# State-space chunks: VectorE adds the product with D behind the sums of y, in place of GpSimd's sum with the part from the state

## What is computed

```python
zxbcdt = u @ in_w.T
z, xBC, dt = jnp.split(zxbcdt, [D_INNER, D_INNER + CONV_DIM], axis=-1)
dt = jax.nn.softplus(dt + dt_bias)
xBC = silu(causal depthwise convolution of xBC with 4 taps, + conv_b)
xh, Bm, Cm = jnp.split(xBC, [D_INNER, D_INNER + D_STATE], axis=-1)
dA = jnp.exp(dt * -jnp.exp(A_log))
state = dA_t * state + (dt_t * x_t) B_t          # for every token t
y_t = state C_t
y = ys + Dp * xh                                  # 32 heads of 32 channels
y = y * jax.nn.silu(z)
y = y * rsqrt(mean(y * y) + EPS) * rms_w
return y @ out_w.T
```

## Time and profile before

| what | value |
|---|---|
| median of 3 runs | 1711.53 us (1709.33 to 1713.68) |
| the profiled execution, its own time | 1710.17 us |
| its span, from the first to the last instruction | 1708.4 us |
| busy: PE, DVE, ACT, POOL | 1363.5, 1109.4, 671.5, 417.0 us |
| mean granted clock of PE | 0.871 of full speed |

### The profile page before, as it was taken

One profiled execution on the slowest core, in us unless ns is written; L12 is line 12 of the kernel. 1 busy time (PEld: TensorE's weight loads), 2 busy tenths in 40 slices (PEclk: granted clock), 3 DMA queues, 4 the chain that ended last, 5 costly groups with the idle time before them and its releaser, 6 DMA issues.

```text
span 1708.4 us, 34435 instructions
## 1 busy us (share of the span) xinstructions
PE 1363.5 (80%) x12846; PEld 928.9 (54%) x12847; DVE 1109.4 (65%) x1669; ACT 671.5 (39%) x1011; POOL 417.0 (24%) x390
## 2 busy tenths in 40 slices
PE   3734889888548989884738999976699999999991
PEld 2214566665345666652425555544477777777770
DVE  3586877887578778876876555556456774667432
ACT  3236434344364343341252111124346664566330
POOL 0122333443313434432132323323100000000004
PEclk9757799999778899987858999885799999999996
DMA  8051000000220000003221000005543553535004
GB/s 293 18 173 61 2 2 1 1 1 1 80 82 2 2 1 1 1 1 105 93 83 50 0 0 0 0 4 209 193 183 142 218 217 114 218 126 219 25 25 153
DMA packets 34029, 132.30 MB, mean 77 GB/s; under 512 B 6665, under 2 KB 8457, under 8 KB 24017
## 3 DMA queue, kind: packets, MB, share of 16 engines
q1 hardware_dynamic: 25808, 103.19, 16.7%
q0 software_dynamic: 8160, 28.32, 4.9%
HBM read 108.82 MB, written 22.68 MB: 77 GB/s over the span
## 4 chain that ended last, share of the span: by engine, by line
PE 57%; DVE 24%; issue 7%; ACT 6%; DMA 4%; POOL 2%; DVEq 0%; POOLq 0%; SPq 0%; ACTq 0%
PE banks L2102 13%; PE banks L2123 13%; DVE mb_ca L592 8%; PE banks L1644 6%; PE banks L1003 5%; PE banks L1721 2%; PE banks L977 2%; PE banks L1040 2%; PE banks L1697 2%; PE banks L1050 2%; PE banks L1051 1%; ACT mb_ca L804 1%; POOL xs_table L2135 1%; DVE mb_xc L604 1%; DVE mb_y_lo L640 1%
## 5 line engine op out<-in xcount | busy, mean ns | idle before, releaser
L2102 PE MATMUL banks<-eb_x_hi,eb_w_hi 128*128 128x128 f16 x1344 | 228.3, 220 | 2.0 <-DVE eb_x_lo L2002 2.0
L2102 PE MATMUL banks<-eb_x_lo,eb_w_hi 128*128 128x128 f16 x1344 | 228.3, 220 | 0.0
L2102 PE MATMUL banks<-eb_x_hi,eb_w_lo 128*128 128x128 f16 x1344 | 228.3, 220 | 0.0
L977 PE MATMUL banks<-mb_u_hi,mb_wi_hi 128*128 (+3 forms) x1152 | 198.0, 220 | 3.3 <-ACT mb_ca L804 3.3
L977 PE MATMUL banks<-mb_u_hi,mb_wi_lo 128*128 (+3 forms) x1152 | 197.7, 220 | 0.0
L977 PE MATMUL banks<-mb_u_lo,mb_wi_hi 128*128 (+3 forms) x1152 | 197.6, 220 | 0.0
L592 DVE SCALAR_TENSOR_TENSOR mb_ca<-mb_xp,mb_par,mb_ca 128x128 f32<-128x128 f32 x384 | 162.9, 487 | 25.3 <-ACT mb_ca L804 23.3
L2102 PEld LDWEIGHTS banks<-eb_x_hi,eb_w_hi 128*128 128x128 f16 x1344 | 132.3, 98 | 4.8 <-issue 2.4
L2102 PEld LDWEIGHTS banks<-eb_x_lo,eb_w_hi 128*128 128x128 f16 x1344 | 132.3, 98 | 2.4
L2102 PEld LDWEIGHTS banks<-eb_x_hi,eb_w_lo 128*128 128x128 f16 x1344 | 132.3, 98 | 0.0
L2123 PE MATMUL banks<-eb_w_hi,eb_h_hi 128*128 x336 | 127.9, 381 | 0.4 <-issue 0.4
(11 more groups left out here) (431 smaller groups left out, 3255.0 us busy)
## 6 DMA issues: line engine op xcount, KB each, us to landing
eb_raw<-e_w SPq DMA_DIRECT2D x36, 1024.0 KB, 4.8
eb_un<-e_w SPq DMA_DIRECT2D x28, 1024.0 KB, 7.2
mb_ring<-m_in_w SPq DMA_DIRECT2D x8, 1072.0 KB, 5.4
xs_table<-zero POOLq DMA_DIRECT2D x1, 6400.0 KB, 21.0
eb_xg<-xs_table POOLq DMA_DIRECT2D x23, 256.0 KB, 2.9
ys_table<-eb_y POOLq DMA_DIRECT2D x21, 256.0 KB, 6.5
ab_raw<-a_in_w SPq DMA_DIRECT2D x4, 1154.0 KB, 11.8
mb_ring<-m_out_w SPq DMA_DIRECT2D x4, 1024.0 KB, 5.3
```

The source lines that it names most:

```text
L977: x = e.matmul(ps[0:width, bank, n * P:(n + 1) * P], a[:, k, f:f + width], b[:, k, ds(i * P, P)], start=(k == 0 and m == 0), stop=(k == KD ...
L2102: o = e.matmul(ps[:, j, c * P:(c + 1) * P], a[:, side, k, f * P:(f + 1) * P], b[:, k, :], start=(k == 0 and m == 0), stop=(k == KD - 1 and ...
```

## The change

The sum of y and `dx` moves from POOL to DVE. Before, POOL added `dx` to `yi` (L941), and DVE's sums L696 and L697 waited for that. Now L696 waits for `yi` itself, and DVE adds `dx` to y in one instruction of 128x1024 behind L697 (L701 of the new file), waits for it, and then multiplies with the gate (L703 of the new file). POOL's L941 goes. Since DVE now reads `dx` late, POOL waits for `yd_done` of the chunk before, before it writes `dx` anew.

```diff
@@ dve, body
                 e.wait_ge(intra_mm, g + 1)
-                e.wait_ge(yid_done, g + 1)
+                e.wait_ge(yi_done, g + 1)
                 e.tensor_tensor(y[:, 0:4, :], ps[:, 7, :].rearrange("p (j t) -> p j t", j=4), yi[:, 0:4, :], ALU.add)
                 e.tensor_tensor(y[:, 4:8, :], ps[:, 2, :].rearrange("p (j t) -> p j t", j=4), yi[:, 4:8, :], ALU.add)\
                     .then_inc(ya_done, 1)
                 e.wait_ge(ya_done, g + 1)
+                e.wait_ge(dx_done, g + 1)
+                e.tensor_tensor(y, y, dx, ALU.add).then_inc(yd_done, 1)
+                e.wait_ge(yd_done, g + 1)
                 e.tensor_tensor(y, y, sz[:], ALU.mult).then_inc(y_done, 1)
@@ pool, body
                 e.wait_ge(xc_done, 2 * (g + 1))
+                if not is_first:
+                    e.wait_ge(yd_done, g)
                 e.tensor_tensor(dx, xc[:], par[:, MB_DCOL:MB_DCOL + JD].unsqueeze(2).to_broadcast([P, JD, P]), ALU.mult)\
                     .then_inc(dx_done, 1)
                 if not is_first:
                     power(g - 1)
                 if not is_last:
                     conv_bc(g + 1)
-                e.wait_ge(dx_done, g + 1)
-                e.wait_ge(yi_done, g + 1)
-                e.tensor_tensor(yi, yi, dx, ALU.add).then_inc(yid_done, 1)
```

More of the change, by code:

```diff
@@ L439, in stage_mamba @@
     diff, exped, m_done = sem("diff"), sem("exped"), sem("m_done")
-    ecum_mm, ec_done, inter_mm, yi_done, yid_done, dx_done = (
-        sem(n) for n in ("ecum_mm", "ec_done", "inter_mm", "yi_done", "yid_done", "dx_done"))
+    ecum_mm, ec_done, inter_mm, yi_done, yd_done, dx_done = (
+        sem(n) for n in ("ecum_mm", "ec_done", "inter_mm", "yi_done", "yd_done", "dx_done"))
     ds_mm, smul, s_done = sem("ds_mm"), sem("smul"), sem("s_done")
```

## The result

The changed kernel takes 1682.03 us (median of 4 runs, 1680.89 to 1686.14). The kernel before, run beside it, takes 1710.43 us (4 runs). The ratio is 0.9833, with a 95% interval of 0.9813 to 0.9852: 28.4 us less. The profiled execution is the slowest of the four, 1686.14 us.

What follows compares the result with a forecast made beforehand. It took VectorE's L592, held by GpSimd's L941 at SBUF access, to keep TensorE waiting. 27.7 + 4.4 - 1.1 + 4.6 us, rounded to 35.6, off 1710.2 gives 1674.6; plus 1.4 for the median, 1676 us, range 1667 to 1686.

Steps and rivals of the forecast that it cites:

- a clock that goes on falling at the chunk's start: Rival: TensorE's clock still falls behind the pause before L1033, so no clock gain; 1680.6 us, chance 0.24.
- The sum L941 goes: Convolution in 14 chunks: without GpSimd's L941 the held L592 ends 2.31 us earlier; gain 27.7 plus 4.4 us.
- The rival that L899 alone keeps the instruction back: Convolution: the long L592 stays and only VectorE's new sum is added; 1712 to 1713 or 1730 us, chance 0.05.
- The price in these 14 chunks is 0: Behind L697: VectorE's new sum costs nothing, since y is ready before y_hi starts; without that cover up to 1.26 us a chunk.
- the clock term: L1033 to first L1003: full TensorE clock saves up to 0.65 us a chunk, 9.1 us in all; half, 4.6 us, taken.
- the cover was gone: Behind L697: the case where y_hi's later start no longer hides VectorE's new sum, costing up to 1.26 us a chunk.
- no fall is left: Case at the chunk's start: TensorE's clock no longer falls, the whole 9.1 us is won; 1671.5 us, chance 0.14.
- The Trainium skill's rule on transposes: L1033 and L1040: transposes don't count as busy for the clock like products, so it would go on falling; gain 31.0 us.
- The last chunks: Each layer's last chunk, without convolution: the new sum loses 1.06 us, covered in layer 2 by the transfer wait; 1.1 us once.
- The collision at the new place: Rival: GpSimd's L928 holds VectorE's new sum by 0.4 us in 14 chunks; +3 us, 1679 to 1684 us, chance 0.12.

Runs made afterwards that it cites:

- a sum that nobody needs: Changed kernel plus a GpSimd 128x1024 sum, dx + dx, at L941's old place, its result awaited by nobody on the path: 1700.01 us.
- the kernel without the sum: Changed kernel with VectorE's sum y + dx removed, leaving out D*x: 1630.01 us, total not comparable; middle chunk period 31.52 us.
- late gates: Changed kernel with the gate products (L616, twice) moved to the next chunk, behind the second L658 and y_lo: 1656.6 us, 1656.23 us when repeated.
- the late GpSimd sum: Kernel before with L941 kept on GpSimd but moved behind the halo copies: 1720.84 us, ratio 1.0084.

## Why the prediction was right, and where it wasn't

1676 us in a range of 1667 to 1686 was forecast; 1682.03 came. The direction and the main mechanism hold, but two terms of the sum were wrong, and both made the gain too large. That the time still lies in the range is in part luck: the forecast nearest to it was that of a clock that goes on falling at the chunk's start (1680.6 us), and what happened was another thing of a like size.

- *The sum L941 goes: right.* The L592 takes 0.89 us where 374.03 - 373.14 = 0.89 was worked out, PE's pause 0.93 us where 0.94 was, the pause of the first chunks gone. From the start of the next projection (L977, now L979) to the next chunk's start a middle chunk takes 19.67 us instead of 21.98, 2.31 less as forecast. That the collision, and not a wait, was the cause is shown by the kernel with a sum that nobody needs. The rival that L899 alone keeps the instruction back is out.
- *"The price in these 14 chunks is 0": this step failed once the clock rose.* I compared the time at which y is ready (385.0) with the time at which `y_hi` starts (386.74), and took the time at which ACT's exponentials are ready as given. When the clock at the chunk's start rose, the exponentials came earlier (in the chunks shown the first starts 2.0 us behind PE's start, where it was 2.8), the idle time before L658 was gone, and DVE's own row of work set `y_lo`. With the clock as it was the step may well have held: in the kernel before, taking 1.3 us of gates out of the same stretch changed nothing. The DVE row that I added up for the clock term as 6.3 us is what happened (6.23); I read it as a bound on a gain and not as the place where the new 1.26 us stand. In the prediction's own words the cover was gone. Against the kernel without the sum it cost 0.77 us of path a chunk, and 1.68 more through the clock.
- *The clock term, 0 to +9.1 us of gain: wrong in kind.* Neither "it falls as before" nor "no fall is left" came. The fall left the chunk's start, which gave 0.9 us with the sum's 0.77 already taken off, and came back in the output projection, where PE has no pause to hide it, for about 1.5 us on average (1.68 against the kernel without the sum). By the chunk it is a loss of 0.6 us instead of a gain of 0.33, and a middle chunk takes 33.97 us where about 33 was forecast. The kernels without the sum and with late gates show that the fall goes when the waiting behind L697 goes, and that 0.93 us before L1035 alone don't bring it. That the longer pauses themselves bring it is argued and not shown: the kernel with L636 behind the product with the gate has the same pauses in twelve chunks and a fall in two.
- *The Trainium skill's rule on transposes* ("TensorE: Matmul & The Clock Gate", Part 4) would have had the clock fall on with the short pause. The trace doesn't bear that out: in the changed kernel, and with late gates, the same transposes stand behind the short pause and the granted clock is 1.00 there in all 14 chunks. So the rule alone doesn't decide it here.
- *The last chunks: right in layer 1, not in layer 2.* In layer 1 L696's wait of 0.20 us is gone, and from L697's start to `y_hi` it takes 3.23 us instead of 1.97: about 1.04 us lost, where 1.06 was worked out. In layer 2 the wait for the kept tokens was to cover it, but it only went from 3.19 to 2.66 us, and the work behind it starts 24.6 us earlier than before, not 25.3: some 0.7 us more, a small term that was put at nothing. What ties the transfer to y isn't settled.
- *The collision at the new place* came only in each layer's first chunk, where L701 takes 1.63 us instead of 1.23, the same 0.4 us as L700 lost there before. The kernel with the statistics L636 moved behind the product with the gate shows that these 0.6 us of L636 are all that kept it away in the middle chunks: without them all 14 sums behind a convolution take 1.62 to 1.63 us. The prediction's reason, that L928 and the sum are both set off by L683, gave the right answer with no room to spare.
- The two profiled executions differ by 23.9 us (1708.4 and 1684.5 us from first to last instruction), close to the stage's 24.6. The medians differ by 28.4, since the profiled execution of the changed kernel was the slowest of four, 4.1 us over their median.

## What to carry to other kernels

When an instruction on VectorE with two inputs in SBUF is many times its usual length and has no wait, look at what GpSimd reads at that moment, and move GpSimd's reading under instructions with at most one input in SBUF (L636, L696 and L697 kept their length beside L928). After a wait is removed, add up again what each engine does from the old wait to the next hand-over: cover that came from a late partner leaves with it. Here the change was worth 28 us, and putting back the cover, by moving work that nobody was waiting for, another 25 to 31 by the medians.

## What the runs showed of the hardware that was not expected

- The collision is over GpSimd's reading only: a GpSimd sum of 1.96 us holds a VectorE instruction with two SBUF inputs, a memset of 0.95 us doesn't. It works both ways: a VectorE sum of 1.22 us made a GpSimd instruction of 0.72 us take 1.65.
- Two reading GpSimd instructions back to back hold two VectorE instructions one after the other (2.00 and 2.12 us for 0.67 and 0.41), while behind a gap of 1.18 us the short one, begun 0.27 us behind GpSimd's, keeps its 0.41.
- How long PE stood at a chunk's start does not alone decide whether the clock falls there. It fell behind a pause of 3.25 us in every middle chunk, behind 2.12 us in nine of twelve, and behind 0.93 us in none. But behind 2.33 us it fell in the kernel before and not with its gates late, and behind 3.04 us, at the end of each layer's first chunk in the kernel with the late GpSimd sum, it didn't fall either. PE at that point, and the stretch behind it (granted clock 1.00):

```profile
201.80 0.21 PE L1033 MATMUL banks<-ident,mb_bcc 32*128 32x32 f32 x1 [3.04 <-DVE mb_quad L697]
...
201.80:205.20 3.40, 3.15 (x19) 1.77 (x19) 3.20 (x5) 1.59 (x4) 0.00 (x0) 1.00 0.02 5
```

- Later in the chunk it fell behind pauses of 0.93, 1.32 and 0.44 us each time, behind 0.34, 0.99 and 0.44 in two of twelve chunks, and behind 0.93, 0.82 and 0.17 in none.
